# Adding the experts' gated outputs to their tokens: one-hot products on TensorE against accumulating indirect DMAs into DRAM

## The reference, cut to what matters

```python
def _L0_ffn_ref(x, gate_query, log_temp, w1, b1, w2, b2):   # x (128, 64, 128), 16 experts
    ...
    gates, idx = jax.lax.top_k(affinity, CAP)                # CAP = 32 tokens for each expert and sequence
    expert_in = jnp.take_along_axis(x[:, None, :, :], idx[..., None], axis=2)
    h = jax.nn.gelu(jnp.einsum('becd,edf->becf', expert_in, w1) + b1[None, :, None, :])
    expert_out = jnp.einsum('becf,efd->becd', h, w2) + b2[None, :, None, :]
    out = jnp.zeros_like(x)
    out = out.at[jnp.arange(b)[:, None, None], idx].add(gates[..., None] * expert_out)
    return out
x = x + jnp.tanh(g_ffn[0]) * _L0_ffn_ref(_layernorm(x, axis=-1), ...)
```

## Time and profile before

| | us |
|---|---|
| three runs | 1919.36, 1921.75, 1922.48 |
| median | 1921.75 |
| profiled execution: span from first to last instruction | 1918.0 |
| first and last gated output (L1803) within that span | 489.9 and 1292.2 |

### The profile page before, as it was taken

The page is one execution under the profiler, slowest core; times in us unless marked ns, Lnnn a source line. Parts: engine busy times, 40 slices in busy tenths (PEclk is TensorE's granted clock), DMA queues, the critical chain, the costliest instruction groups (busy, mean ns, idle before and its releaser), DMA issues. The chain is left out here.

```text
span 1918.0 us, 72744 instructions
## 1 busy us (share of the span) xinstructions
PE 1812.8 (95%) x28635; PEld 1311.9 (68%) x28635; DVE 1609.1 (84%) x3645; ACT 1564.4 (82%) x2773; POOL 662.4 (35%) x918
## 2 busy tenths in 40 slices
PE   6999998896999999999999999998999999999898
PEld 4777776542666666666666666766777777777677
DVE  5999987598788888888888888778999999988744
ACT  5899997575998989898989989876888888888543
POOL 4788887231000000000000000004666666655565
PEclk8999999897999999999999999999999999999899
DMA  7644545495000000000000001004665555533233
GB/s 180 130 99 93 103 94 102 139 364 187 14 11 15 13 14 11 15 13 15 10 14 14 13 12 52 2 2 107 153 169 154 144 156 147 154 69 72 64 111 121
DMA packets 312954, 160.67 MB, mean 84 GB/s; under 512 B 236558, under 2 KB 295862, under 8 KB 312374
## 3 DMA queue, kind: packets, MB, share of 16 engines
q1 hardware_dynamic: 312278, 157.95, 31.4%
q10 hardware_dynamic: 480, 0.05, 0.0%
HBM read 62.33 MB, written 36.83 MB: 52 GB/s over the span
## 5 line engine op out<-in xcount | busy, mean ns | idle before, releaser
L1793 DVE TENSOR_TENSOR h<-g,h 128x1024 f16<-128x1024 f32 x256 | 313.3, 1224 | 138.3 <-ACT h L1725 138.0
L239 PEld LDWEIGHTS psE<-ew,h 128*128 128x128 f16 x6144 | 351.2, 98 | 56.0 <-issue 40.1
L239 PE MATMUL psE<-ew,h 128*128 128x128 f16 x6144 | 365.2, 219 | 12.8 <-DVE eo L1803 6.0
L1720 ACT ACTIVATE g<-psH,eb1T 128x512 f32<-128x512 f32 x512 | 330.2, 680 | 30.9 <-PE psH L239 24.5
L814 POOL TENSOR_TENSOR Ph<-E,Ph 128x512 f16<-128x512 f32 x192 | 222.0, 1156 | 235.9 <-ACT Ph L768 235.9
L1866 POOL MEMSET rbias<- 64x384 f32 x1 | 0.4, 411 | 839.2 <-POOLq L133 839.2
L1725 ACT ACTIVATE h<-g 128x1024 f16<-128x1024 f32 x256 | 270.6, 1057 | 8.1
L720 ACT ACTIVATE vB<-psV 128x512 f16<-128x512 f32 x384 | 225.9, 589 | 51.2 <-PE psV L618 49.0
L841 DVE TENSOR_TENSOR vB<-psV,vB 128x512 f16<-128x512 f32 x384 | 248.4, 678 | 1.1 <-ACT vB L720 1.0
L618 PE MATMUL psV<-shared 96*64 96x512 f16 x1536 | 209.9, 379 | 1.5 <-DVE vB L841 1.5
L820 POOL TENSOR_TENSOR E<-E,rden 128x512 f32<-128x512 f32 x192 | 199.7, 1040 | 15.1 <-DVE rden L852 14.3
(11 more groups left out here) (308 smaller groups left out, 3417.9 us busy)
## 6 DMA issues: line engine op xcount, KB each, us to landing
keys_ahead<-shared SPq DMA_DIRECT2D x52, 512.0 KB, 4.8
shared<-keys_ahead SPq DMA_DIRECT2D x52, 512.0 KB, 3.6
rawe<-in_L_ffn_w_dram SPq DMA_DIRECT2D x32, 256.0 KB, 3.1
wb<-rw SPq DMA_DIRECT2D x64, 128.0 KB, 2.0
rows<-places SPq DMA_DIRECT2D x110, 64.0 KB, 2.5
out_dram<-x SPq DMA_DIRECT2D x7, 512.0 KB, 3.2
context_T<-shared SPq DMA_DIRECT2D x64, 48.0 KB, 2.4
PT<-Ph SPq DMA_TRANSPOSE x192, 2.8
```

The source lines that it names most:

```text
L239: last = e.matmul(to, a, b, start=start and n == 0, stop=stop and n == 2, **flags)
L1720: e.activation(g32[:, ft, :], psH[:, ft, :], ACT.Gelu_apprx_tanh, bias=b1T[:, a.expert(1) * FT + ft:a.expert(1) * FT + ft + 1]).then_inc(s ...
L1793: e.tensor_tensor(h[:, 1 - par, 1, 2 * q:2 * q + 2, :], g32[:, 2 * q:2 * q + 2, :], h[:, 1 - par, 0, 2 * q:2 * q + 2, :], ALU.subtract)\
```

## The change

The gated outputs no longer go through PE. Each group of 16 sequences gets a tensor of 1024 rows of 128 f32 in DRAM (`sums`). The gate of the block is now multiplied into `gate_slot`, and `tok_slot` becomes `row_slot`, a 32-bit row number in `sums`, made by three DVE instructions of 128x512 in place of two at the end of `select_tokens`. Ahead of a group the 8 bias products alone go into `psA`, `residual` adds them to x, and SP copies the 8 tiles to `sums` (`seed`, 512 KB). Then for each expert POOL issues four indirect DMAs, one for each block of 128 rows of `eo32`, that add these rows to the rows of `sums` named by `row_slot`. Behind the last expert of a group, SP copies `sums` back to x (`back`, 512 KB). An expert's four DMAs are issued once its outputs are gated and all four DMAs of the expert before have landed. `eo32` has three buffers; DVE reuses one when its DMAs have landed.

```diff
-                    e.tensor_copy(gate_slot[:], psG[:])
-                    e.tensor_scalar(tok_slot[:], psI[:], block_of_p[:], None, ALU.add)
+                    e.wait_ge(s["idx16"], 1)
+                    e.tensor_scalar(idx32[:], psI[:], block_of_p[:], None, ALU.add).then_inc(s["rows_of_slots"], 1)
+                    e.tensor_scalar(gate_slot[:], psG[:], gate, None, ALU.mult)
+                    e.wait_ge(s["rows_of_slots"], 1)
+                    e.tensor_tensor(row_slot[:], idx32[:], slot_base[:].unsqueeze(1).broadcast_to([P, NE, B // 4]),
+                                    ALU.add)
...
+            def landed(eng, n):
+                eng.wait_ge(s[f"landed{n % OUTS}"], 16 * RT * (n // OUTS + 1))
...
+                    def seed(G):
+                        e.wait_ge(s["xadd"], G + 1)
+                        e.dma_start(tiles_of(G)[1], tiles_of(G)[0]).then_inc(s["seeded"], 16)
+                    def back(G):
+                        landed(e, NE * G + NE - 1)
+                        e.dma_start(tiles_of(G)[0], tiles_of(G)[1]).then_inc(s[f"back{G % 2}"], 16)
                     load_shares(0)
                     for k in range(EARLY, NT):
+                        if k % GT == 3 and k // GT >= 2:
+                            back(k // GT - 2)
                         if k % GT == 3:
                             load_shares(k // GT)
                         body(Step(None, 0, k))
+                        if k % GT == 1:
+                            seed(k // GT - 1)
+                    seed(NG - 1)
+                    back(NG - 2)
...
+                    back(NG - 1)
+                    e.wait_ge(s["back1"], 16 * (NG // 2))
...
+                @block.gpsimd
+                def _(e):
+                    for n in range(NE * NG):
+                        G, k = divmod(n, NE)
+                        e.wait_ge(s["gated"], n + 1)
+                        if n:
+                            landed(e, n - 1)
+                        if k == 0:
+                            e.wait_ge(s["seeded"], 16 * (G + 1))
+                        for r in range(RT):
+                            to_rows = bass.IndirectOffsetOnAxis(ap=row_slot[:, k, RT * G + r:RT * G + r + 1], axis=0)
+                            e.indirect_dma_start(out=sums[G], out_offset=to_rows, in_=eo32[:, n % OUTS, r, :],
+                                                 in_offset=None, compute_op=ALU.add)\
+                             .then_inc(s[f"landed{n % OUTS}"], 16)
...
+                        if a.e == 9 and a.G + 1 < NG:
+                            biases(a.G + 1)
...
-                            for r in range(RT):
-                                for hl in range(2):
-                                    for bp in range(2):
-                                        rows = slice(64 * bp, 64 * bp + 64)
-                                        last = e.matmul(psA[:, bp, r, :], put[rows, r, :], eo[rows, hl, r, :],
-                                                        start=False,
-                                                        stop=a.e == NE and hl == 1, skip_group_check=True)
-                            last.then_inc(s["A"], 1)
...
-                                e.activation(eo[:, 0], eo32[:], ACT.Copy).then_inc(s["eo_hi"], 1)
...
                         if a.has(-1):
+                            n = NE * a.G + a.e - 1
                             wait(e, s["E"], j - 1)
-                            wait(e, s["eo_lo"], j - 2)
+                            if n >= OUTS:
+                                landed(e, n - OUTS)
...
-                            for r in range(RT):
-                                e.tensor_scalar(put[:, r, :], iota[:],
-                                                tok_slot[:, a.expert(-1), a.group(-1) * RT + r:a.group(-1) * RT + r + 1],
-                                                None, ALU.is_equal).then_inc(s["put"], 1)
...
-                            e.tensor_tensor(eo[:, 1], eo32[:], eo[:, 0], ALU.subtract)\
-                             .then_inc(s["eo_lo"], 1)
...
+                        if a.e == 14 and a.G + 1 < NG:
+                            residual(a.G + 1)
+                        if a.G > 0 and 6 <= a.e < 6 + GT:
+                            G = a.G - 1
+                            e.wait_ge(s[f"back{G % 2}"], 16 * (G // 2 + 1))
+                            queue_stats(e, flat(G, GT, a.e - 6))
```

More of the change, by code:

```diff
@@ L30 @@
 AHEAD = 52
+GB = 16
+NGROUPS = B // GB
 EPS = 1e-5
@@ L146, in _build @@
     block_of_p = sb(whole, "block_of_p", [P, 1], F32)
-    iota = sb(whole, "iota", [P, P], F16)
+    slot_base = sb(whole, "slot_base", [P, B // 4], F32)
     eps_col = sb(whole, "eps_col", [P, 1], F32)
@@ L174, in _build @@
     places = nc.dram_tensor("places", [B, NE * CAP], F16).ap()
+    sums = [nc.dram_tensor(f"sums_{n}", [GB * N, D], F32).ap() for n in range(NGROUPS)]
     folds = [nc.dram_tensor(name, [DC, 2, 2, 8 * D], F16).ap() for name in ("fold_keys", "fold_values")]
@@ L1190, in select_tokens @@
             ROUNDS = CAP // 8
[L1191 removed]
+            i32 = row_slot[:]
             vals = sb(c, "vals", [P, NE, CAP], F32)
@@ L1615, in _, with biases @@
                     wait(e, s["g_1"], Step(None, 0, GT - 1), 2)
+                    def biases(G):
+                        if G:
+                            e.wait_ge(s["xadd"], G)
+                        e.wait_ge(s["weigh"], 96 * (G + 1))
+                        for r in range(RT):
+                            for bp in range(2):
+                                rows = slice(64 * bp, 64 * bp + 3 * NE)
+                                last = e.matmul(psA[:, bp, r, :], weigh[rows, r, :], b2[rows], start=r == 0,
+                                                stop=r == RT - 1, skip_group_check=True)
+                        last.then_inc(s["bias"], 1)
+                    biases(0)
                     def body(a):
@@ L1711, in body @@
                                 e.activation(xn[:, tpar, 0], xnf[:, tpar], ACT.Copy).then_inc(s["x_hi"], 1)
-                            if ft == 2 and a.has(-1):
-                                wait(e, s["gated"], j - 1)
-                                wait(e, seeded["A"], j - 2)
-                                e.activation(eo[:, 0], eo32[:], ACT.Copy).then_inc(s["eo_hi"], 1)
                             if a.has(1):
@@ L1728, in _ @@
                     all_steps(e, body)
-                    e.activation(g32[:, 0, 0:1], zero_col[:], ACT.Exp, bias=zero_col[:])
+                    e.activation(warm[:], zero_col[:], ACT.Exp, bias=zero_col[:])
                     e.wait_ge(s["nmr"], 1)
@@ L1806, in body @@
                             queue_tile(a.t + 1, (a.k + 1) % 2)
-                        if a.e == 1 and a.G > 0:
-                            residual(a.G, -1)
-                        if a.has(-1):
-                            wait(e, seeded["A"], j - 2)
-                            for r in range(RT):
-                                e.tensor_scalar(put[:, r, :], iota[:],
-                                                tok_slot[:, a.expert(-1), a.group(-1) * RT + r:a.group(-1) * RT + r + 1],
-                                                None, ALU.is_equal).then_inc(s["put"], 1)
                         h_low(0)
-                        if a.has(-1):
-                            wait(e, s["eo_hi"], j - 1)
-                            e.tensor_tensor(eo[:, 1], eo32[:], eo[:, 0], ALU.subtract)\
-                             .then_inc(s["eo_lo"], 1)
                         if next_tile:
```

56 lines of the change are left out of this document (17 added, 39 removed).

## The result

The changed kernel takes 2415.1 us (median of 4 runs, 2410.29 to 2416.58), the one before 1920.72 us (4 runs). The ratio is 1.257, 95% interval 1.255 to 1.259: 494 us slower, where 135 us were forecast. The direction and the mechanism held, the size did not, and the time lies outside the range of 1855 to 2275 us.

A forecast was written before the change was run, and what follows sets the result against it. PE was taken to bound the kernel before, POOL's DMA loop the changed one: 128 x 7.3 us plus 6.2 us, less 805.9 us, gives +134.7 us, so 2056 us, 7% slower; range 1855 to 2275 us.

The forecast's parts named there:

- What bounds, and the worth of what goes: Experts' stage: PE is the bound, ACT close behind; a scatter that costs nothing would be worth 72 us.
- The loop and who waits for it: POOL's issues and landing form a chain; DVE's gating waits for it, PE for DVE; it decides above 5.75 us a step.
- T: Time of POOL's loop for one expert's four indirect DMAs, 4 x I + L; set at 7.3 us, ends 3.3 and 10.8.
- I: Time POOL needs for one indirect DMA issue; set at 1.2 us, ends 0.444 and 1.7 us.
- L: Time from the end of POOL's last issue to POOL seeing it landed; set at 2.5 us, ends 1.5 and 4.0.
- Hiding: Rival: POOL's loop stays below 5.75 us and PE sets the pace; 62.4 us faster, 1859 us; chance 0.25.
- The dearer loop: Rival: T at 9 us or more, from a read and write per row or PE's lower clock; 2338 us; chance 0.13.
- POOL and DVE: Experts' stage: DVE's 2-port instructions `sel` and `xnfe` would keep POOL from making descriptors and lengthen T; no size given.
- The smaller terms: Stage's head and end: 3 us more at the head, 3.2 us for the last copy back.

The follow-up runs named there:

- f_no_scatter: The kernel before without the one-hot put, the f16 parts of the gated outputs and the scatter products, nothing in their place; 1847.8 us, ratio 0.962.
- e_two_sums: The changed kernel with odd experts adding into a second tensor, so POOL waits for the DMAs of two experts before; 2136.1 us.
- d_one_block: The changed kernel with one in place of four indirect adding DMAs per expert; 1866.2 us.
- d_two_blocks: The changed kernel with two in place of four indirect adding DMAs per expert; 1912.3 us.
- b_no_add: The changed kernel with the indirect DMAs writing their rows in place of adding them; 2119.2 us.
- j_low_one: The changed kernel with the low part of h made by a DVE instruction with one source in SBUF in place of two; 2378.7 us.
- g_plain_pool: The changed kernel with plain DMAs of 128 rows issued by POOL to fixed rows, without row numbers and without add; 1872.0 us.

## Why the prediction was wrong

**What bounds, and the worth of what goes: right.** PE's scatter and its helpers were worth 73 us, forecast 72 (f_no_scatter). That it is so close is in part luck: the forecast held 730 us for 128 steps, 5.70 us each, against 802.3 us for 127, and the step came out at 5.78 us.

**The loop and who waits for it: right.** T = 4 x I + L sets the pace once it is above PE's step. e_two_sums took L out and nothing else appeared; d_one_block and d_two_blocks put the loop on both sides of the edge; DVE waited for DMAs 523.8 us and PE for DVE 359.0 us, as laid out.

**L: right in size.** 2.5 us set, 2.54 us measured. Its make-up was not what I argued. The add's part is 0.45 us, and without it L is 2.09 us, above the 1.5 us that I gave to a write alone. Part of it is no transfer: DVE waits for the same landing and starts 1.8 us after the last issue, POOL some 0.64 us after DVE (medians over the stage). No run separates that part further.

**I: wrong, and this is the step that failed.** "I set I = 1.2 us", from POOL's elementwise 1.156 us and SP's transpose of 1.232 us. POOL spends 845.6 / 512 = 1.65 us in an issue and 131.9 / 512 = 0.26 us between issues, 1.91 us in all. Four times the difference of 0.71 us is 2.8 us, times 128 it is 363 us, and the miss is 2415 - 2056 = 359 us. Even my high end of 1.70 us was too low. With the measured T of 10.11 us the prediction's own formula gives 128 x 10.11 - 799.7 = +494 us, as measured. Its parts, by the runs: 0.54 us for a plain DMA from POOL, 0.42 us for row numbers, 0.58 us for the add; 0.30 us ahead of every issue that follows another; and 0.11 us on average (1.652 - 1.543) by which some issues are lengthened. The trace of before had a row for the first alone, SP's 0.48 us. The duration of an elementwise instruction on POOL, 1.156 us, told nothing of an issue there: by form that takes 0.54 to 1.54 us.

**The rivals.** Hiding (0.25) was out by more than 4 us a step. Its time, 1859 us, was near what the runs that do hide show, 1866 and 1872 us. By the rule of the Trainium skill beside it (DMA: Bandwidth & Descriptors, "Anatomy of one DMA — SWDGE (gpsimd) path") the estimate was T = 5.15 us; the trace disagrees for the indirect adding form with 10.11 us. The plain form did hide, as that estimate says, with issues of 0.54 us for the estimate's 1 us. The dearer loop (0.13, T at 9 us or more, 2338 us) is what happened, in part by the first of its two reasons, that every row needs a read and a write: b_no_add has a T of 7.8 us, so the add took T from there past 9 us, and row numbers and gaps had it above 7.3 us already. Its second, PE's lower clock, came as well (0.85, 48 products in 4.46 us), but does not set the pace: PE still waits 2.49 us for DVE in the same step. It cost at most the 66.4 - 35.2 = 31 us in which POOL waited for DVE.

**POOL and DVE.** The prediction named the Trainium skill's rule on 2-port instructions (SBUF — State Buffer, "Who interferes with whom") and expected `sel` and `xnfe` to be in the way. In the changed kernel no issue starts inside `sel`, and the 47 that start inside `xnfe`, all within 0.05 us of its start, are not lengthened. Of the 128 lengthened issues 127 started inside the low part of h, which has two sources in SBUF. The same section of the Trainium skill says that such an instruction is in the way of a GpSimd instruction that reads SBUF; the trace agrees for indirect issues, at 0.34 to 0.42 us in most of those lengthened, 0.4 us a step. So the rule that I had chosen was not the one at work in this kernel, but that is a matter of when the issues start: in e_two_sums 52 issues start inside `sel` and 14 of them are lengthened, by 0.07 to 0.15 us, again by what was left of it less 0.13 us. j_low_one shows a one-source form in the place of the low part in the way too.

**The smaller terms** were 3 us at the head and 3.2 us at the end. At the head the first gated output comes 491.6 - 489.9 = 1.7 us later and POOL's first issue follows it by 0.34 us. At the end 6.7 us pass between the last issue and the next stage; 2.5 us for the landing, 3.2 us for the copy and the 1 us that stood there before make the same. g_plain_pool, with all of them and a step of 5.86 us, is 24 us above f_no_scatter; 0.08 x 128 = 10 us of it are the step, and I have not accounted for all of the rest.

## What to carry to other kernels

Moving work to an idle engine turns a throughput into a chain when the new work must be ordered: count issues per step times the issue's time, plus the wait for the landing, and hold it against the step, before counting what is saved. An issue that no row of the trace shows should be measured by itself first; here 1.9 us against 1.2 us was the whole error. When such a chain is longer than a step, it can be given every second step: the same DMAs that cost 494 us for all experts save 29 us for seven of sixteen.

## What the runs showed of the hardware

- POOL's undisturbed issue of a 64 KB DMA of 128 rows, median: 0.54 us plain, 0.96 us with row numbers, 1.54 us with row numbers and add; 1.40 us with 64 rows in place of 128.
- An indirect DMA of 128 rows with add went out as 144 packets, one of 64 rows as 80; 128 rows without add as 32, indirect or plain.
- From the end of the last of four such issues to POOL's next: 2.5 us with the add, 2.1 us without.
- Indirect issues are 0.30 us apart on POOL even when nothing is waited for; plain ones follow at once.
- An indirect issue that started while DVE's low part of h (128x1024, two sources in SBUF) was under way, with over 0.2 us of it left, lost what was left, less 0.13 us, 127 of 127 times; 63 that started within 0.03 us of its start lost nothing. Of 256 plain issues that started inside it one took longer than 0.6 us.
- With a one-source low part (128x1024) 110 issues ended some 0.08 us after a low part that had begun after they did, at 1.63 or 1.86 us.
